# One expert layer of a two-layer cross-attention and mixture-of-experts kernel: rows sorted by expert through DRAM instead of every expert on every row

## What is computed

```python
scores = xn @ w_router.T                      # xn: rms norm of the layer norm, 2048 rows x 128
scores_topk, idx = jax.lax.top_k(scores, 2)   # 2 of 8 experts for each row
weights = softmax(scores_topk)
up = moe_linear(xf, ids, w_up)                # row i: 128 -> 512 with the weights of its expert
u, gate = split(up, 2)
h = u * silu(gate)                            # 256 values
down = moe_linear(h, ids, w_down)             # 256 -> 128 with the weights of its expert
out = sum(down * weights, over the 2 experts) + skip
```

## Time and profile before

| | |
|---|---|
| three runs | 592.29, 592.91 (median), 593.42 us |
| profiled execution, its own time | 593.19 us |
| its span, first to last instruction | 591.4 us |
| PE busy | 528.8 us, 89% of the span |
| DVE busy | 398.6 us, 67% |
| ACT busy | 285.3 us, 48% |
| POOL busy | 143.0 us, 24% |
| mean granted TensorE clock | 0.965 of full speed |
| DMA | 10.78 MB, 18 GB/s mean |

### The profile page before, as it was taken

One profiled execution on the slowest core, in us unless ns is written; L12 is line 12 of the kernel. 1 busy time (PEld: TensorE's weight loads), 2 busy tenths in 40 slices (PEclk: granted clock), 3 DMA queues, 4 the chain that ended last, 5 costly groups with the idle time before them and its releaser, 6 DMA issues.

```text
span 591.4 us, 12949 instructions
## 1 busy us (share of the span) xinstructions
PE 528.8 (89%) x3952; PEld 412.8 (70%) x3952; DVE 398.6 (67%) x1306; ACT 285.3 (48%) x841; POOL 143.0 (24%) x376
## 2 busy tenths in 40 slices
PE   3899999897999969899999999778999999874996
PEld 1444444485566647788888888667999999762875
DVE  4389998966488974656656556547777877727553
ACT  0588989852565624342322223125665766732221
POOL 3232222110387771000121102120123322231000
PEclk9999999999899998899999999978999999996899
DMA  5900002001000000000000000000000000000001
GB/s 118 350 30 11 12 8 61 1 1 29 4 6 3 2 2 1 1 1 0 2 1 2 0 0 0 0 2 2 1 1 1 1 0 0 0 1 1 18 19 35
DMA packets 20447, 10.78 MB, mean 18 GB/s; under 512 B 7468, under 2 KB 18998, under 8 KB 20406
## 3 DMA queue, kind: packets, MB, share of 16 engines
q1 hardware_dynamic: 17750, 9.10, 5.5%
q10 hardware_dynamic: 2656, 1.18, 0.7%
HBM read 9.09 MB, written 1.18 MB: 17 GB/s over the span
## 4 chain that ended last, share of the span: by engine, by line
PE 76%; DVE 9%; issue 5%; ACT 4%; POOL 3%; DMA 1%; SPq 1%; DVEq 0%; POOLq 0%; ACTq 0%
PE psum L1225 10%; PE psum L1374 9%; PE psum L1179 6%; PE psum L1362 5%; PE psum L1363 5%; PE psum L1364 5%; PE psum L1415 4%; PE psum L1333 4%; PE psum L1446 4%; PE psum L1406 4%; PE psum L1426 3%; PE psum L1487 2%; PE psum L1212 2%; PE psum L1316 2%; PE psum L1474 1%
## 5 line engine op out<-in xcount | busy, mean ns | idle before, releaser
L569 ACT ACTIVATE work<-psum 128x512 f32<-128x512 f32 x64 | 38.1, 597 | 76.4 <-PE psum L1364 76.4
L500 ACT ACTIVATE wa<-psum,negmax 128x120 f32<-128x120 f32 x256 | 67.8, 376 | 10.5 <-DVE negmax L811 10.4
L1031 DVE TENSOR_TENSOR work<-psum,work 128x512 f32<-128x512 f32 x64 | 44.1, 691 | 31.4 <-PE psum L1364 25.5
L1225 PE MATMUL psum<-wa 32*128 32x480 f32 x128 | 63.1, 1082 | 2.1 <-ACT wa L500 2.0
L1374 PEld LDWEIGHTS psum<-dnT,work 128*128 128x128 f32 x512 | 62.0, 191 | 2.7
L1374 PE MATMUL psum<-dnT,work 128*128 128x128 f32 x512 | 62.3, 275 | 0.0
L597 ACT ACTIVATE work<-work,d 128x120 f32<-128x120 f32 x128 | 48.7, 381 | 21.7 <-DVE d L1103 21.7
L1041 DVE SCALAR_TENSOR_TENSOR x<-psum,gate,x 128x128 f32 (+1 forms) x128 | 36.1, 344 | 33.0 <-PE psum L1374 32.9
L1362 PE MATMUL psum<-x_hi,up_hi 128*128 128x512 f32 (+1 forms) x128 | 54.6, 426 | 2.6 <-DVE work L1031 2.3
L683 POOL TENSOR_TENSOR rstd<-mv,eps 128x1 f32<-128x1 f32 x32 | 6.1, 190 | 206.2 <-DVE mv L941 206.1
L1363 PE MATMUL psum<-x_lo,up_hi 128*128 128x512 f32 (+1 forms) x128 | 51.7, 404 | 0.0
(11 more groups left out here) (231 smaller groups left out, 1139.9 us busy)
## 6 DMA issues: line engine op xcount, KB each, us to landing
x<-in_x_dram ACTq DMA_DIRECT2D x4, 256.0 KB, 5.2
work<-in_L_ffn_w_down_dram SPq DMA_DIRECT2D x1, 1024.0 KB
wa<-mscratch SPq DMA_DIRECT2D x64, 2.0 KB
out_dram<-wa SPq DMA_DIRECT2D x4, 256.0 KB, 2.3
wa<-in_ctx_dram SPq DMA_DIRECT2D x16, 60.0 KB, 1.8
work<-in_L_xattn_Wq_dram SPq DMA_DIRECT2D x1, 512.0 KB
work<-in_L_xattn_Wk_dram SPq DMA_DIRECT2D x1, 512.0 KB
work<-in_L_xattn_Wv_dram SPq DMA_DIRECT2D x1, 512.0 KB
```

The costliest lines, as they stand in the source:

```text
L500: e = nc.scalar.activation(prob[:, z, hh, :], psum[:, 3 + 2 * half + h // 4, (h % 4) * LK:(h % 4 + 1) * LK], ACT.Exp, bias=negmax[:, z, hh ...
L1031: nc.vector.tensor_tensor(hT[:, e % 2, j, :], psum[:, 2 * j, :], silu[:, j, :], ALU.mult).then_inc(c_h, 1)
L1225: m = nc.tensor.matmul(psum[:, 3 + g, 0:4 * LK], qs[rows, z, :], kexp[rows, z].rearrange("p i k -> p (i k)"), start=True, stop=True)
```

## The change

Stage C no longer computes every expert on every row. Rows are handled in two halves of 8 sequences (1024 rows, so 2048 pairs of row and expert in each half).

- A DRAM area `by_expert` of 18,432 rows of 512 B holds, for each half, one region of 1024 rows for each expert and a spare one. SP writes zeros over all of it in stage A, in 8 DMAs of 2304 rows, between the loads of the context.
- DVE finds the two experts of each row (`pick_experts`), PE counts with small bf16 products how many earlier rows chose the same expert (`rank`), and DVE makes the row numbers (`place_rows`) and a table of the tiles (`tile_table`): each expert's rows are cut in tiles of 128, at most 23 tiles for a half. For the first half this is done in steps 14 and 15 of stage B, for the second between B and C.
- POOL sends the rows to their places with 16 indirect DMAs of 128 rows for each half (`scatter`).
- Stage C is 46 tiles. SP reads the tile's first row from the table to a register and loads 128 rows (`load_tile`), PE reads the expert's number to a register, turns the tile (line 1413), makes one plain fp32 product of 512 columns (line 1646), turns the 256 hidden values in two pieces and makes two fp32 products of 128 columns (line 1663). ACT does the silu and one copy, DVE one product and two copies. SP stores the tile where it came from (`store_tile`).
- POOL gathers the two results of each row (2 indirect DMAs for a sequence), and DVE adds them to `x` with their weights. For the first 8 sequences this goes along with tiles 30 and later, for the last 8 with the first steps of stage D.
- Removed are the split of the up weights and of `x` in stage B, a copy of K on POOL for each sequence in stage B, a copy of the context on POOL in stage D, and the 256 gated additions of stage C. The pipelines of B and D are written out in full (`peel=NB`) instead of half as loops.

The core of the diff:

```diff
+            AHEAD = 3
+            for n in range(AHEAD):
+                load_tile(n)
+            for n in range(TILES):
+                if n + AHEAD < TILES:
+                    load_tile(n + AHEAD)
+                store_tile(n)
...
+            def load_tile(n):
+                h, i = n // TILES_H, n % TILES_H
+                if i == 0:
+                    sp.wait_ge(k_tab, h + 1)
+                    sp.wait_ge(scattered[h], 16 * SLOTS_H)
+                if n >= RING_C:
+                    sp.wait_ge(ct_xt, n - RING_C + 1)
+                row = sp.value_load(tile_tab[0:1, h, 1, i:i + 1], min_val=0, max_val=2 * ROWS_H - P)
+                tile_rows[n] = row
+                sp.dma_start(ct_x[:, n % RING_C, :], by_expert[bass.ds(row, P), :]).then_inc(ld_ct[n % RING_C], 16)
+
+            def store_tile(n):
+                sp.wait_ge(ct_ye, n + 1)
+                sp.dma_start(by_expert[bass.ds(tile_rows.pop(n), P), :], ct_y[:, n % RING_C, :]).then_inc(st_ct[n % RING_C], 16)
...
+            for h in range(2):
+                for i in range(SLOTS_H):
+                    scatter(h, i)
+                weight_exp(h)
...
+            def ct_result(n):
+                dve.wait_ge(ct_dn, n + 1)
+                if n >= RING_C:
+                    dve.wait_ge(st_ct[n % RING_C], 16 * (n // RING_C))
+                nc.vector.tensor_copy(ct_y[:, n % RING_C, :], psum[:, 4, 0:D]).then_inc(ct_ye, 1)
...
+            tile_pipeline([(0, lambda n: ct_turned(n) if n < TILES else None), (1, ct_product), (3, ct_result),
+                           (0, lambda n: c_tail(lambda late: c_step(n, late), 2))])
...
+            def ct_turn(n):
+                h, i = n // TILES_H, n % TILES_H
+                if i == 0:
+                    pe.wait_ge(k_tab, h + 1)
+                tile_expert[n] = pe.value_load(tile_tab[0:1, h, 0, i:i + 1], min_val=0, max_val=NE - 1)
+                pe.wait_ge(ld_ct[n % RING_C], 16 * (n // RING_C + 1))
+                if n:
+                    pe.wait_ge(ct_xe, n)
+                turn(psum[:, 2, 0:P], ct_x[:, n % RING_C, :], P).then_inc(ct_xt, 1)
...
+            tile_pipeline([(0, lambda n: ct_turn(n) if n < TILES else None), (1, ct_up_project), (2, ct_turn_hidden),
+                           (3, ct_down_project), (0, lambda n: c_part(c_logits, c_step(n, 5))),
+                           (0, lambda n: c_part(c_turn, c_step(n, 3)))])
```

More of the change, by code:

```diff
@@ L78, in software_pipeline @@
 def software_pipeline(eng, stages, n=NB, peel=4):
-    assert all(lag <= peel - 2 for lag, _ in stages) and (n - peel) % 2 == 0
+    assert peel == n or all(lag <= peel - 2 for lag, _ in stages) and (n - peel) % 2 == 0
     def step(b, parity):
@@ L89, in software_pipeline @@
         step(b, b % 2)
-    with eng.Fori(0, (n - peel) // 2) as i:
-        for parity in range(2):
-            step(i * 2 + (peel + parity), parity)
+    if n > peel:
+        with eng.Fori(0, (n - peel) // 2) as i:
+            for parity in range(2):
+                step(i * 2 + (peel + parity), parity)
     for b in range(n, n + peel):
@@ new lines, in ct_halves, with ct_tail @@
+            def ct_halves(n):
+                if n == ROUND_TILE:
+                    nc.scalar.copy(vo_hi[:, :, :], vo1[:, :, :]).then_inc(rounded, 1)
+                    act.wait_ge(ld_late, 16 * (N_LATE + 1))
+                    nc.scalar.copy(w1_hi[:, :], ew1.rearrange("p n f -> p (n f)")).then_inc(rounded, 1)
+                    nc.scalar.copy(rows_r[:, :, :], expert_rows).then_inc(rounded, 1)
+            def ct_tail(n):
+                for late, stage in ((4, tail_evict("c")), (6, tail_scores("c"))):
+                    b = c_step(n, late)
+                    if b is not None:
+                        stage(b, b % 2)
@@ L735, in _, with gather, c_tail @@
                                     ).then_inc(halved, 1)
-            with pool.Fori(1, GROUPS) as g:
-                c_tails(g)
+            def gather(b):
+                h, r = b // HALF_B, b % RING_C
+                if b % HALF_B == 0:
+                    for s in range(RING_C):
+                        pool.wait_ge(st_ct[s], 16 * len(range(s, (h + 1) * TILES_H, RING_C)))
+                if b >= RING_C:
+                    pool.wait_ge(c_added, b - RING_C + 1)
+                for j in range(2):
+                    i = j * HALF_B + b % HALF_B
+                    nc.gpsimd.indirect_dma_start(y_rows[:, r, j, :], None, by_expert[:, :],
+                                                 bass.IndirectOffsetOnAxis(rows_at[:, h, i:i + 1], 0)).then_inc(ld_y[r], 16)
+            def c_tail(at, of):
+                if of <= at < of + HALF_B:
+                    gather(at)
+                for late, stage in ((0, tail_rstd), (2, tail_keep)):
+                    if of <= at - 1 - late < of + HALF_B:
+                        stage("c")(at - 1 - late, (at - 1 - late) % 2)
+            for k in range(HALF_B + 3):
+                c_tail(k, 0)
             def d_stage(b, z):
```

596 lines of the change are left out of this document (384 added, 212 removed).

## The result

The changed kernel took **798.0 us** (795.8 to 799.0, 4 runs) against 593.2 us of the kernel before on the same chip: a ratio of 1.345, 95% interval 1.342 to 1.349. The forecast was 763 us, slower, and the time lies in the range given. So the direction and the mechanism of stage C were right, and the sum was 35 us short. The profiled execution has a span of 795.3 us.

A forecast was written before the change was run, and what follows sets the result against it. Stage C was taken as bound by a closed loop of store and load, not by PE: first tile 252, first loads 10, 42 loops x 6.65 = 279, last tile 9, then 211; span 761, forecast 763 us, range 695 to 828.

The forecast's parts named there:

- The closed loop: Stage C: load n+4 waits for store n, so steps do not overlap; 42 loops at 6.65 us, 279; chance 0.58.
- Rival 5: Stage C: loads are there in time, a step about 2.0 us, not slower; time 563 us; chance 0.04.
- The length of the ring: Stage C, one loop for one tile: 5.45 us at the high clock, 6.95 at the low one.
- table read and registers: SP's read of the tile's row from SBUF to a register, in each loop: taken as 0.7 us, between 0.1 and 1.8.
- The clock: PE in stage C: mostly at the 1.2 GHz level, one step in five at the high level, so 6.65 us a loop.
- Rival 2: Stage C: the closed loop at the high clock, 5.45 us a loop; time 704 us; chance 0.17.
- The first tile: Start of stage C: first tile at 252 us, behind 16 scatters on POOL at 1.3 each, 21 us.
- The zeros: Stage A: 9.4 MB of clears cost 0, at most 3 us if they hold up the context of sequence 4.
- Rival 4: Start of stage C: scatters bound it at 2.8 us each, 24 us more; time 785, up to 815; chance 0.08.
- Tiles 0 to 4: Start of stage C: first four loads land together, 3 x 3.4 = 10 us, then a loop of 6.65.
- The tail of C: End of stage C: the last tile still needs three shorter steps, 9 us, so D starts at 550.
- D and E: From D's start to the end: 204 us, plus 6 for longer steps (7.7 to 8.4) and 1 for a gather: 211.

The follow-up runs named there:

- f_fill: The changed kernel with three more unused matrix products a tile on PE, ahead of the turn: 756.2 us, ratio 1.273.
- e3: The changed kernel with only GpSimd's order in the last attention stage changed (context split and norm root ahead of the late gathers): 776.3 us, ratio 1.310.
- c2_hold: The kernel of four edits together (c1_all), with the second half's scatters sent only when five tiles are done: 582.5 us, ratio 0.982.
- g_row: The changed kernel with SP's table read for the next load put ahead of the store of tile n: 762.9 us, ratio 1.287.
- d_nogather: The changed kernel with GpSimd's changed order (e3), and the second half's 16 gathers left out: 791.9 us, ratio 1.338.
- c1_all: The changed kernel with 8 loaded-tile buffers and loads seven ahead, GpSimd's changed order, late first clears and eight early scatters: 576.8 us, ratio 0.973.
- a2_hold: The changed kernel with GpSimd's second-half scatters held back until five tiles' results are copied: 787.6 us, ratio 1.330.
- e1 to e4: Single edits to the changed kernel: loads one tile further ahead (615.1 us), 8 buffers with loads seven ahead (579.2), GpSimd's order (776.3), first clears later (781.6).
- e4: The changed kernel with the first two 512 KB clears moved behind the loop of context loads: 781.6 us, ratio 1.316.

## Why the prediction was right, and where its sum was off

**The closed loop** is what happened: each turn of a tile waits for the load, the load for the store, the store for the down product. Loads one tile further ahead halved it and more, loads seven ahead removed it. Rival 5 (loads are there in time) describes what the change would have been with that order: it gave 563 us, the run with 8 buffers took 579.

**The length of the ring.** Forecast 6.95 at the low level and 5.45 at the high one; f_fill measured 6.78 and 5.42 in one trace. By pieces, at the low level: PE and DVE 3.9 (4.0), store 0.35 with hand-overs (0.4), table read and registers 0.78 (0.7), landing 1.82 (1.8, from the context loads of the earlier trace rows). The read itself is 0.28. The Trainium skill, "DMA: Bandwidth & Descriptors", section "Latency and other measured facts", gives some 600 ns as its floor; this trace does not agree, and the rest of the 0.7 that I took lies in SP's register work behind the read. **The clock** was low in nearly every ring and not in four of five: 6.84 instead of 6.65, over 41 rings 7.6 us. Rival 2 (high clock) did not come, though the ring at that clock was sized right.

**The first tile** came at 254.4 (252). GpSimd's 16 scatters start 1.26 us apart (1.3 taken), 0.96 busy and 0.30 between. The zeros cost stage A 3.1 where I took 0 and named 3 as the bound with its place, the context of sequence 4; the scatters gave 0.7 of it back. Rival 4 (scatters at 2.8) did not come. The Trainium skill, "SBUF — State Buffer", section "A bandwidth-pool intuition that's wrong (but worth ruling out)", would have made a scatter 3.1 us beside VectorE's copies. No run shows that, and none is a full test of it. In the last one, eight scatters lie in a stretch in which DVE was busy for 12.5 of 20 us, and took GpSimd 0.95 to 1.24 us each; but DVE made sums and scalings there and no plain copy, and the trace does not show when a single scatter landed. The stretch, and the longest of them:

```profile
210.00:230.00 20.00, 12.45 (x159) 8.92 (x151) 12.46 (x55) 4.06 (x11) 12.70 (x20) 0.71 0.08 27
```
```profile
211.91 1.24 POOL L848 DMA_INDIRECT by_expert<-scored,rows_at  x1 [0.20 <-issue]
```

**Tiles 0 to 4** took 21.35 us where the sum has 10 + 6.65. Two errors of opposite sign stand behind that. Without a stall, these tiles take 9.8 us (e3: up products at 255.6 and 265.4), 7 less than I counted; and the stall, which no part of the prediction foresaw, adds 11.5. Net 4.7.

**The tail of C** took 11.3 us (9), 2.3 more; PE was busy for 10.7 of them, at a granted clock of 0.65.

**D and E** took 228.0 us where I had 211: this is the step of the sum that failed, half of the 34 us. I costed the second half's tail in D by its busy time on DVE and PE, 0.7 us a step, as if D's step were the work of its busiest engine. From the first sequence's context products to the last's D takes 140.2 us (572.3 to 712.4), and took 116.0 before (392.4 to 508.4). These 24.2 us are all that the last stages grew, and I had 7. The base was a little short too: 7.7 is the distance of one pair of rows, and the steps before are 7.6 to 8.5 from the third on. Three pieces can be told apart:

- About 4.4 us are the ring of DVE and POOL: five steps of 10.6 to 10.9 us became 9.8 when GpSimd's order was changed.
- About 3 us are the clock, for which D's terms had nothing. One step took 12.9 us (597.2 to 610.1), and from 598 to 605 its products ran at the low level. With GpSimd's order changed the same step is 12.9 us in e3, where the clock fell in it too, and 9.8 in c2_hold, where it stayed up. First a part of that step in the changed kernel, then c2_hold's:

```profile
602.00:604.00 2.00, 2.00 (x7) 1.57 (x7) 0.81 (x3) 0.33 (x1) 0.56 (x1) 0.50 0.26 66
```
```profile
386.00:396.00 10.00, 8.73 (x68) 8.22 (x69) 7.66 (x23) 5.57 (x21) 1.99 (x7) 1.00 0.01 2
```

- Some 16 us are left when both are gone: c2_hold takes 131.8 us from the first context products to the last, with steps of 9.8 and then 8.5. The rows of e3 above give this to hand-overs between DVE and PE, whose orders interlock. No run tested that second ring, and its cause stays argued.

2.4 + 4.7 + 7.6 + 2.3 + 17.0 is the whole difference of 34 us between the sum's 761 and the span of 795.3. Two small slips in the working changed little: PE's terms at the low level add up to 3.86 and not to 3.7 to 3.8 (the trace has the loop's first part at 3.9), and 24 us on top of 763 are 787 and not 785.

## What to carry to other kernels

Loads that are said to run n tiles ahead have to be followed through the queue that issues them: behind a store that waits for tile n's last product, a load three ahead in a pipeline of four steps is not ahead at all. Compare the number of steps between first and last use of a tile with the distance of the loads before anything else is tuned; here that number, with the buffers that it needs, was worth 219 us of 798.

A serial ring can cost twice, by its length and by TensorE's granted clock, which was at the 1.2 GHz level in it: 1.4 of 6.8 us here. And work that is added to a tuned pipeline is to be priced by who waits for whom in each engine's order, not by the busy time that it adds.

## What was not expected of the hardware

While GpSimd sent 16 scatters back to back (1.26 us apart), other engines stood still for 4 to 11 us at a time in six of the eleven different kernels with such a burst: the changed one (and again when it was run once more), f_fill, g_row, d_nogather, c1_all and c2_hold; a2_hold lost 3.4 us in one ring. In the four others (e1 to e4) nothing happened beside the same burst, although none of their edits touches it. When the burst was moved the stall moved (252.8 to 266, then 265.5 to 284.4), when it was spaced out it was gone, and 13 us with it. So the burst has to do with it, and is not enough. What the engines wait for is not in the trace (it names "remote" and "issue" there). That it has to do with code that is run for the first time, as the expectation of a2_hold has it, was tested by no run; the cause stays open.

TensorE's granted clock averaged over a stretch is no measure of the clock at which it worked in the rings: in e3 it reads 0.75 over 276 to 547, in the changed kernel 0.52, with rings of the same 6.8 us. In both the products ran at the 0.50 level, and what differs is the reading while PE stood idle. First e3, then the changed kernel with PE idle:

```profile
404.00:405.00 1.00, 0.00 (x0) 0.00 (x0) 0.00 (x0) 0.00 (x0) 0.00 (x0) 1.00 0.18 53
...
406.00:407.00 1.00, 0.01 (x1) 0.01 (x1) 0.00 (x0) 0.00 (x0) 0.00 (x0) 0.92 0.22 66
407.00:408.00 1.00, 1.00 (x2) 0.67 (x3) 0.29 (x1) 0.00 (x0) 0.00 (x0) 0.50 0.00 0
408.00:409.00 1.00, 1.00 (x2) 0.23 (x1) 0.00 (x0) 0.00 (x0) 0.00 (x0) 0.50 0.00 0
```
```profile
404.00:405.00 1.00, 0.00 (x0) 0.00 (x0) 0.00 (x0) 0.00 (x0) 0.00 (x0) 0.50 0.19 55
```

At the ends of the stage it did matter. Where executions of one kernel differ in this reading, those at 0.86 were 5 to 7 us shorter than those at 0.76 to 0.77: 774.1 to 776.4 against 780.5 us in e3, 778.5 against 784.3 in e4, 782.3 and 785.7 against 789.6 and 791.6 in a2_hold. The changed kernel was only ever seen at the lower reading (0.76 to 0.78). In the traces, 3.5 us of the difference lie where C goes over to D. At the lower reading (changed kernel, e4) the third last store follows the fourth last by 4.1 us, and D's first context products follow the last store by 5.6 to 5.7; at the higher one (e3, a2_hold) it is 2.3 and 4.0. So some us of what the medians of e3, e4 and a2_hold gain against the changed kernel are this and not their edit. Why an execution reads one or the other is not known.
